# Query and key weights between the pieces of x, their bias apart, fewer wake-up transposes

## The reference

```python
xn = layernorm(x)                                  # no scale, no shift
q, k, v = (xn @ W + b per head for each of the three)
y = softmax(q @ k.T * 16 ** -0.5 + causal) @ v     # per head
attention = concat(y) @ Wo + bo
top2, selected = top_k(xn @ Wr, 2); p = softmax(top2)
experts = sum over e of p[e] * ((clip(silu(xn @ Wg[e]), -7, 7) * (xn @ Wu[e])) @ Wd[e])
out = x + attention + experts
```

## Time and profile before

| | us |
|---|---|
| median of 3 runs | 441.28 |
| lowest and highest | 441.12, 441.63 |
| span of the profiled execution | 440.0 |
| total of the profiled execution beside its span | not given on the page |
| PE busy | 422.0 |
| DVE busy | 314.2 |
| ACT busy | 237.6 |
| POOL busy | 194.6 |

### The profile page before, as it was taken

How to read it: one execution, slowest core, us unless ns; L and a number is a source line. 1 busy time by engine, 2 the same in 40 slices (tenths; PEclk the granted TensorE clock), 3 DMA queues, 4 the chain that set the end, 5 groups by cost and what they waited for, 6 DMA issues and landing times.

```text
span 440.0 us, 8430 instructions
## 1 busy us (share of the span) xinstructions
PE 422.0 (96%) x2851; PEld 255.2 (58%) x2851; DVE 314.2 (71%) x1019; ACT 237.6 (54%) x551; POOL 194.6 (44%) x223
## 2 busy tenths in 40 slices
PE   8898979989999999999999999999999999999896
PEld 8486425656364366557666676565655664756333
DVE  6827999999888835885577735867576768591485
ACT  1563363433647665655564546646555547464992
POOL 5331256585054277346744256233743365212410
PEclk9999959998999999999999999999999999999999
DMA  7289896788076249435784069621893454110582
GB/s 237 70 218 201 277 207 182 257 280 269 4 150 181 83 135 230 154 118 187 184 233 175 23 187 221 189 87 50 245 256 107 145 155 153 21 38 3 169 310 97
DMA packets 40373, 71.34 MB, mean 162 GB/s; under 512 B 5893, under 2 KB 30598, under 8 KB 40332
## 3 DMA queue, kind: packets, MB, share of 16 engines
q0 software_dynamic: 9360, 39.99, 28.8%
q1 hardware_dynamic: 27132, 26.76, 24.5%
q10 hardware_dynamic: 3840, 4.08, 3.6%
HBM read 55.85 MB, written 15.60 MB: 162 GB/s over the span
## 4 chain that ended last, share of the span: by engine, by line
PE 72%; DVE 18%; issue 3%; DMA 3%; POOL 2%; ACT 1%; SPq 0%; ACTq 0%
PE psum L1364 15%; PE psum L1307 14%; PE psum L1268 11%; PE psum L1287 11%; PE psum L1373 7%; DVE psum L1004 5%; DVE mxa L1007 5%; PE psum L1223 3%; PE psum L1199 3%; PE psum L1347 2%; DMA bqk<-in_bqk 2%; PE psum L1316 2%; PE psum L1354 2%; DVE resid L976 1%; POOL probs L823 1%
## 5 line engine op out<-in xcount | busy, mean ns | idle before, releaser
L896 ACT ACTIVATE probs<-psum 128x512 f32<-128x512 f32 (+1 forms) x320 | 151.5, 575 | 38.6 <-PE psum L1287 37.8
L1004 DVE CUSTOM_DVE_ANT_0 psum<-psum,maskrow 128x128 f32<-128x128 f32 (+3 forms) x256 | 121.4, 505 | 18.1 <-PE psum L1268 17.8
L1268 PE MATMUL psum<-packk,packq 96*128 96x512 bf16 (+3 forms) x384 | 93.3, 328 | 2.5 <-DVE mxa L1004 1.2
L1007 DVE TENSOR_REDUCE mxa<-psum 128x1 f32<-128x512 f32 x128 | 87.7, 685 | 9.4 <-PE psum L1268 9.2
L1287 PE MATMUL psum<-packq,packk 99*128 99x512 bf16 (+3 forms) x384 | 90.5, 332 | 2.9 <-ACT probs L896 2.7
L1307 PE MATMUL psum<-probs,v 128*32 128x512 f32 (+3 forms) x768 | 76.1, 502 | 2.2 <-POOL probs L823 1.8
L823 POOL TENSOR_SCALAR_AFFINE_SELECT probs<-probs 128x512 f32<-128x512 f32 (+1 forms) x48 | 40.0, 836 | 64.1 <-ACT probs L896 63.6
L1268 PEld LDWEIGHTS psum<-packk,packq 96*128 96x128 bf16 x384 | 34.5, 97 | 54.7 <-issue 16.8
L1287 PEld LDWEIGHTS psum<-packq,packk 99*128 99x128 bf16 x384 | 33.0, 98 | 45.1 <-issue 12.7
L790 POOL DMA_INDIRECT xg<-xn_rows,token x39 | 37.6, 965 | 45.9 <-PE psum L1354 35.9
L1166 DVE SCALAR_TENSOR_TENSOR tanh<-tanh,psum 128x256 f32<-128x256 f32 x39 | 16.3, 417 | 49.8 <-ACT tanh L931 49.5
(11 more groups left out here) (127 smaller groups left out, 477.2 us busy)
## 6 DMA issues: line engine op xcount, KB each, us to landing
qk_parts<-stage SPq DMA_DIRECT2D x24, 256.0 KB, 2.9
stage<-expert_rows SPq DMA_DIRECT2D x16, 256.0 KB, 4.1
packq<-qk_parts SPq DMA_DIRECT2D x16, 192.0 KB, 4.6
packk<-qk_parts SPq DMA_DIRECT2D x14, 192.0 KB, 6.1
x<-in_x SPq DMA_DIRECT2D x4, 512.0 KB, 5.3
packq<-qk_parts SPq DMA_DIRECT2D x16, 128.0 KB, 6.2
xn_rows<-probs ACTq DMA_DIRECT2D x4, 512.0 KB, 14.5
out<-x SPq DMA_DIRECT2D x16, 128.0 KB, 2.5
```

What stands on the lines that cost most here:

```text
L896: act.activation(probs[:, g % RING, h, 0:width], psum[:, bank, 0:width], ACT.Exp, scale=SCALE)\
L1004: ins = dve.tensor_tensor_reduce(out=chunk, in0=chunk, in1=maskrow[:, BANK - width:], scale=1.0, scalar=NEG, op0=ALU.add, op1=ALU.max, acc ...
L1007: ins = dve.tensor_reduce(into, chunk, op=ALU.max, axis=AX.X)
L1268: pe.matmul(psum[:, bank, 0:width], packq[0:MAXROW, u % SLOTS, i // HALF, h, P * (i % HALF):P * (i % HALF + 1)], packk[0:MAXROW, u % SLOTS ...
```

## The change

The planner's jobs and the code change together:

- WARM goes from 60 to 52.
- The query and key weights are issued by SP, not ACT, and wait for nothing. Their due time puts them after the second piece of x in SP's list, and the due times of the pieces are now -10 to -7 rather than all -10.
- Their bias alone stays with ACT, at the start of its list, and counts on a semaphore of its own, `bqk_in`. PE's first projection waits for `wqk_in` at 16, ACT's first evacuation for `bqk_in` at 16.
- wvr, bv, wo and bo go to SP's queue, behind the pieces of x.
- A projection's first half is declared to come after the first transposed chunk only, its second half after the second, and PE's waits are split likewise. The first half's lag is 0, so the planner may put the second right behind it. The transposes of the second piece are due at 1 rather than 10.

```diff
--- before.py
+++ after.py
@@ -249,7 +249,7 @@
 LAST_DUE = 40000
 RATE = 280
 SMALL = 65536
-WARM = 60
+WARM = 52
 PACE = dict(attention=(60000, 425000), experts=(90000, 375000))
 
 
@@ -278,25 +278,26 @@
         job("POOL", ("const", n), ns, due=due)
     job("SP", ("ones",), 500, [("POOL", ("const", 1))], due=2000, lag=2000, size=73728)
     for q in range(4):
-        job("SP", ("x", q), 500, lag=2000, due=-10, size=524288)
-    job("ACT", ("weights_qk",), 950, [("SP", ("x", 1))], due=-50, lag=2000, size=540000)
-    job("ACT", ("weights_v",), 2200, [("ACT", ("weights_qk",))], due=-50, lag=2000, size=820000)
+        job("SP", ("x", q), 500, lag=2000, due=q - 10, size=524288)
+    job("SP", ("weights_qk",), 500, due=-8.5, lag=2000, size=524288)
+    job("ACT", ("bias_qk",), 2000, due=-60, lag=2000)
+    job("SP", ("weights_v",), 2000, due=-5, lag=2000, size=820000)
     for q in range(4):
         job("DVE", ("stats", q), 1900, [("SP", ("x", q))], due=10 * q)
         job("POOL", ("rstd", q), 960, [("DVE", ("stats", q))], due=-20)
         job("DVE", ("ln", q), 1280, [("POOL", ("rstd", q))], due=10 * q - 5)
         job("ACT", ("ln", q), 420, [("DVE", ("ln", q)), ("SP", ("load", 0, 0, 0))], due=34000 + q, lag=2000, size=524288)
         for c in range(DC):
-            pe(("xnt", q, c), 436, [("DVE", ("ln", q))], due=10 * q, takes=("xnt", q, c))
+            pe(("xnt", q, c), 436, [("DVE", ("ln", q))], due=10 * q if q > 1 else q, takes=("xnt", q, c))
             job("ACT", ("xnt", q, c), 478, [("PE", ("xnt", q, c))], due=10 * q, frees=("xnt", q, c))
 
     for k in range(QKS):
         b, grp, op, n = qk_tile(k)
         w = k // 2
         due = 10 * n + 6 + op if k < 4 else 25000 + 1500 * (k - 4)
-        after = [("ACT", ("xnt", 2 * b + n, c)) for c in range(DC)] + [("ACT", ("weights_qk",))]
-        pe(("qk1", k), 853, after, due=due, takes=("qk", k))
-        pe(("qk2", k), 853, [("PE", ("qk1", k))], due=due - 1)
+        after = [("ACT", ("xnt", 2 * b + n, 0)), ("SP", ("weights_qk",))]
+        pe(("qk1", k), 853, after, due=due, takes=("qk", k), lag=0)
+        pe(("qk2", k), 853, [("PE", ("qk1", k)), ("ACT", ("xnt", 2 * b + n, 1))], due=due - 1)
         job("ACT", ("hi", k), 570, [("PE", ("qk2", k))] + ([("SP", ("store", w - 2))] if w >= 2 else []), due=due)
         job("DVE", ("resid", k), 662, [("ACT", ("hi", k))] + ([("POOL", ("lo", k - 2))] if k >= 2 else []), due=due,
             frees=("qk", k))
@@ -307,7 +308,7 @@
 
     for t in range(NT):
         due = 10000 + 600 * t
-        pe(("v", t), 884, [("ACT", ("xnt", t // 4, c)) for c in range(DC)] + [("ACT", ("weights_v",))] + ([("DVE", ("v_ones",))] if t == 0 else []),
+        pe(("v", t), 884, [("ACT", ("xnt", t // 4, c)) for c in range(DC)] + [("SP", ("weights_v",))] + ([("DVE", ("v_ones",))] if t == 0 else []),
            due=due, takes=("v", t))
         job("ACT", ("v", t), 325, [("PE", ("v", t))], due=due, frees=("v", t))
         if t == 0:
@@ -330,7 +331,7 @@
     dve(("experts",), 1600, [("DVE", ("tiles", 1))], 20005)
     dve(("list",), 1300, [("PE", ("list",))], 20006, frees=("list",))
     dve(("gates",), 750, [("ACT", ("gates",))], 30000)
-    dve(("widen",), 228, [("DVE", ("v_ones",)), ("DVE", ("ln", 3)), ("ACT", ("weights_v",))], 12000)
+    dve(("widen",), 228, [("DVE", ("v_ones",)), ("DVE", ("ln", 3)), ("SP", ("weights_v",))], 12000)
     pe(("bias",), 853, [("DVE", ("widen",))], 30000, takes=("bias",))
     dve(("bias",), 425, [("PE", ("bias",))], 30000, frees=("bias",))
     for t in range(NT):
@@ -576,6 +577,7 @@
         freed = [sem(f"freed{i}") for i in range(BANKS)]
         x_in = [sem(f"x_in{q}") for q in range(4)]
         wqk_in = sem("wqk_in")
+        bqk_in = sem("bqk_in")
         wvr_in = sem("wvr_in")
         wo_in = sem("wo_in")
         fetch_in = [sem(f"fetch_in{i}") for i in range(WSLOTS)]
@@ -663,6 +665,15 @@
                 sp.dma_start(x[:, span_rows(q), :],
                              x_d[P * 4 * q:P * 4 * (q + 1), :].rearrange("(t p) d -> p t d", p=P)).then_inc(x_in[q], 16)
 
+            def load_qk_weights():
+                sp.dma_start(wqk[:, :, :, :], wqk_d).then_inc(wqk_in, 16)
+
+            def load_v_weights():
+                sp.dma_start(wvr[:, :, :], wvr_d).then_inc(wvr_in, 16)
+                sp.dma_start(bv[:, :], bv_d).then_inc(wvr_in, 16)
+                sp.dma_start(wo[:, :, :], wo_d).then_inc(wo_in, 16)
+                sp.dma_start(bo[:, :], bo_d.partition_broadcast(P)).then_inc(wo_in, 16)
+
             def spread_ones():
                 sp.wait_ge(consts, 2)
                 sp.dma_start(packk[MAXROW:KROWS, :, :, :, :].rearrange("p s c h t -> p (s c h t)")
@@ -720,7 +731,7 @@
                     wait_freed(sp, ("proj", t))
                 sp.dma_start(out_d[P * t:P * (t + 1), :], x[:, t, :]).then_inc(out_done, 16)
 
-            walk("SP", {"x": load_x, "ones": spread_ones, "store": store, "load": load, "neg": neg_rows, "z_load": load_z, "out": store_out})
+            walk("SP", {"x": load_x, "weights_qk": load_qk_weights, "weights_v": load_v_weights, "ones": spread_ones, "store": store, "load": load, "neg": neg_rows, "z_load": load_z, "out": store_out})
             sp.wait_ge(out_done, 16 * NT)
 
 
@@ -829,16 +840,8 @@
 
         @block.scalar
         def _(act):
-            def load_qk_weights():
-                act.wait_ge(x_in[1], 16)
-                act.dma_start(wqk[:, :, :, :], wqk_d).then_inc(wqk_in, 16)
-                act.dma_start(bqk[:, :, :], bqk_d).then_inc(wqk_in, 16)
-
-            def load_v_weights():
-                act.dma_start(wvr[:, :, :], wvr_d).then_inc(wvr_in, 16)
-                act.dma_start(bv[:, :], bv_d).then_inc(wvr_in, 16)
-                act.dma_start(wo[:, :, :], wo_d).then_inc(wo_in, 16)
-                act.dma_start(bo[:, :], bo_d.partition_broadcast(P)).then_inc(wo_in, 16)
+            def load_qk_bias():
+                act.dma_start(bqk[:, :, :], bqk_d).then_inc(bqk_in, 16)
 
             def store_xn(q):
                 act.wait_ge(xn_ready, 4 * (q + 1))
@@ -861,7 +864,7 @@
                 _, grp, op, n = qk_tile(k)
                 w = k // 2
                 if k == 0:
-                    act.wait_ge(wqk_in, 32)
+                    act.wait_ge(bqk_in, 16)
                 bank = wait_filled(act, ("qk", k))
                 if w >= 2:
                     act.wait_ge(qk_out[w % 2], 16 * PARTS * (w // 2))
@@ -936,7 +939,7 @@
                     act.wait_ge(scatter_out[i % 2], 16 * (i // 2))
                 act.mul(yo[:, i % 2, :], psum[:, bank, 0:D], 0.5).then_inc(freed[bank], 1)
 
-            walk("ACT", {"weights_qk": load_qk_weights, "weights_v": load_v_weights, "load": load_first_k, "ln": store_xn, "xnt": copy_xnt, "v": copy_v, "hi": qk_hi_part, "mid": qk_mid_part, "gates": gates, "exp": exps,
+            walk("ACT", {"bias_qk": load_qk_bias, "load": load_first_k, "ln": store_xn, "xnt": copy_xnt, "v": copy_v, "hi": qk_hi_part, "mid": qk_mid_part, "gates": gates, "exp": exps,
                          "y": copy_y, "yt": copy_yt, "half_yt": copy_yt_half, "xgt": copy_xgt, "tanh": silu_gate, "yo": copy_yo})
 
 
@@ -1202,14 +1205,16 @@
             def project_qk_first(k):
                 b, grp, op, n = qk_tile(k)
                 if k == 0:
-                    pe.wait_ge(wqk_in, 32)
+                    pe.wait_ge(wqk_in, 16)
                 if grp == op == 0:
-                    for c in range(DC):
-                        wait_freed(pe, ("xnt", 2 * b + n, c))
+                    wait_freed(pe, ("xnt", 2 * b + n, 0))
                 wait_room(pe, ("qk", k))
                 qk_product(k, 0)
 
             def project_qk(k):
+                b, grp, op, n = qk_tile(k)
+                if grp == op == 0:
+                    wait_freed(pe, ("xnt", 2 * b + n, 1))
                 qk_product(k, 1).then_inc(filled[FILL_AT[("qk", k)][0]], 1)
 
             def project_v(t):
```

## The result

| us | before | changed |
|---|---|---|
| median, 11 executions each | 441.80 | 445.58 |
| lowest and highest | 441.12, 444.11 | 443.81, 447.67 |
| span of the profiled execution | 440.0 | 443.2 |

What follows compares the result with a forecast made beforehand. PE was taken as the bound from 120 us on, with a DVE stage before it. Gains of 1.64 + 0.34 = 2.0 us at the start cut the 440.0 span to 438.0; plus 1.3 gave 439.3, range 436.8 to 442.3.

Steps and rivals of the forecast that it cites:

- Bias and weights (1.64): Before the first projection: PE's 1.64 us wait for the bias goes entirely, the weights landing in time.
- Eight transposes fewer (0.34): At the start on PE: eight fewer wake-up transposes bring the first projection 0.34 us earlier (bounds 0 and 0.76).
- rival C: At the start: small bias rows delay x's first piece by up to 2.7 us; 442.0 us, chance 0.05.
- Pieces of x, other weights, order of the halves: Around the first projections: later pieces and moved weights cost nothing, PE gains nothing, first store up to 2.8 us earlier.
- The sum: First projection 2.0 us earlier, carried through DVE's full stage and PE to the end: 439.3 us, chance 0.47.
- the largest unknown: After the start: the planner's shifted clock can change later orders where two jobs were close; no size of its own.
- Rival B: Near 40 us: ACT's blocked stores make PE stand up to 2.7 us more; 442.0 or 444.1 us, chance 0.13.
- Rival A: Before the DVE stage: DMA landings set its start, the 2.0 us become waiting; 441.3 us, chance 0.19.
- Rival D: At 54 to 56 us or PE's stall: hole filled or stall gone, some 2 us more won; 437.3, chance 0.16.
- The last sign of being wrong: Between 20 and 120 us: the forecast is wrong if the planner's order opens new holes in PE.
- The 1.3 us beside the span: Outside the profiled span of 440.0: 1.3 us up to the runs' median, taken as unchanged by the change.

Runs made afterwards that it cites:

- e2: The kernel before with only the bias put on a semaphore of its own; 441.33 us, ratio 0.9992.
- second trace: The changed kernel run and profiled again, unaltered; median 445.39 us, ratio 1.0080, this profiled execution 443.73 us.
- e6: All the change's transfers, semaphores, waits and 52 transposes, in the engine order of the kernel before; 440.56 us, ratio 0.9987.
- e7: As e6, but ACT also waits for the second piece of x before issuing the bias; 440.19 us, ratio 0.9975.
- e3: The changed kernel with the four stores of normalised rows moved from ACT's to SP's queue; 442.76 us, ratio 1.0021.

## Why the prediction was wrong

*Bias and weights (1.64): right.* PE's wait is gone; the weights landed at 7.4 as forecast, the bias well before 8.6. That the weights in ACT's queue are there at 11.25 held in the trace that was read, not in e2 (13.45).

*Eight transposes fewer (0.34): zero.* The term was not summed rightly: its own parts give 11.86 (10.99 + 0.87), not 12.05. The transposes of xn now begin at 10.11 and wait 0.36 and 0.30 for DVE, and the projection starts at 12.40, when they had ended before (12.39). DVE took up the first piece 0.43 later (4.73, not 4.30). In the second trace DVE was in time (4.36), but there the 52 transposes themselves took 8.83 us, longer than the 60 before (8.64), and the projection starts at 12.41. Over twelve traces 52 of them took 7.25 to 8.84, a spread wider than the 0.76 that eight are worth. With the bias early DVE began at 4.32 to 5.26 over twelve traces, without it 4.21 to 4.35 over four: rival C's mechanism may be there, at 0 to 0.9, and is no cause of the loss.

*Pieces of x, other weights, order of the halves: right, but for the first store.* The third piece is taken up at 11.33 with no idle DVE, v waits for no weight, the first evacuation is at 14.39 (forecast 14.2). The first store came at 20.68, 1.23 earlier and not in the 18.5 to 20 that was forecast: it needs the second tile too, whose remainder (19.27) stands in DVE's new list behind the rows of the third and fourth piece (15.84 + 3.50).

*The sum: the failing step.* "DVE's full stage (from 42.37 in the chain) therefore starts 2.0 earlier" took the order behind the start as unchanged, and took a lead at the start to come through whole. In the chain that stage begins at 44.48, and at 41.75 in the second trace, not near 40.4, and with four more score tiles to do. The text named the order as the largest unknown, and still gave it no term; the range's upper end came from single blocks alone. The trace where the clock stayed, set against that of before, gives the account that was needed: before 441.7; start -1.6, +1.7 up to the first set (`resid 0`, v's place, and some 0.4 that the old order loses as well, as e6 shows), POOL beside the negation +1.7 up to the second, +0.1 after, in all +1.9 to 2.0 (396.38 against 394.42): 443.7, as measured. The fall of the clock puts the median 1.8 above that. With the order kept, e6 shows what the second half of the step was worth: 1.1 us of a lead of 1.87 reach the end.

*Rival B: the place, not the mechanism.* ACT's block kept its length, and PE's stall rose to 2.31, below the 3.4 from which B was to decide. What counted was how much work for DVE stood ahead of the stall. *Rival A* has some truth: at 35.81 all but 0.22 of the lead is gone, to list order and not to landings, and in e6, in the old order, 0.39 of 1.87 goes by the first set, with the stall behind ACT's block at 1.93 and not 1.45. *Rival D* is reversed: the hole near 40 grew, and the clock fell behind it. The last sign of being wrong, new holes in PE between 20 and 120 us, is the one that came: 1.58 at 97 us.

The 1.3 us beside the span was low as well (1.7 in the second trace, 443.73 against 442.0; 1.9 to 2.0 in the runs of before); a changed kernel that did all that was forecast would have shown 439.7 to 440.0. e7 and e6, at 440.2 and 440.6, come nearest.

## What to carry to other kernels

Where a planner writes all the lists from declared times, a small change to the times is a change to every list: set the two written lists side by side before summing, and look at what each moved entry stands next to, on its own engine and on the engine that it disturbs. Test a change of transfers in the old order first. An early start is worth what still stands of it at the next stall, and that is read from the work queued ahead of the stall.

## What had not been expected of the hardware

- Small VectorE instructions (128 x 16, 0.17 us) took 0.67 to 1.06 while GpSimd worked on SBUF, an indirect DMA's issue among it, and were back at 0.17 to 0.18 when GpSimd was held for 1.28 us.
- After one hole of PE near 40 us the granted clock fell in six traces to 0.57 to 0.66 over 4 us (most of it at the lower level, 1.2 GHz; holes of 1.91 to 2.57) and stayed at 1.00 in five (holes of 1.90 to 2.46), in both ways for one and the same kernel; the fall cost 1.3 us at the first set of the changed kernel. What decides it was not found.
- One transfer's issue held ACT for 4.2 to 4.7 us in every order, where the three before it took 0.4 to 0.5 each; moved to SP's queue, the four were issued in 9.50 us (e3).
